# Second block of a two-block window-attention kernel: MLP input turned ahead of the attention mix, next group's input turned behind the projection, x1 in two buffers

## Chip, core and metric

The kernel runs on 1 core of one Trainium2 chip. The metric is the device time of one execution in microseconds (us). In the text, TensorE is PE, VectorE is DVE, ScalarE is ACT, GpSimd is POOL, and SyncE, which only issues DMAs here, is SP.

## What is computed

Two transformer blocks in a row over 32 images of 56 x 56 pixels with 96 channels, in float32. The first (swin) has shifted windows of 7 x 7 and normalises behind its branches. The second, which the change touches, is this:

```python
def _L1_conv_ref(x, g1, b1, w_qkv, b_qkv, w_proj, b_proj, g2, b2, w_fc1, b_fc1, w_fc2, b_fc2):
    shortcut = x
    xn = layernorm(x, g1, b1)
    windows, Hp, Wp = window_partition(xn, WS)       # WS = 8: windows of 64 pixels
    attn_out = attention(windows, w_qkv, b_qkv, w_proj, b_proj)   # 6 heads of 16
    attn_out = window_unpartition(attn_out, WS, Hp, Wp, H, W)
    x = shortcut + attn_out
    h = layernorm(x, g2, b2)
    h = jax.nn.gelu(jnp.einsum('bhwc,cd->bhwd', h, w_fc1) + b_fc1, approximate=False)
    h = jnp.einsum('bhwc,cd->bhwd', h, w_fc2) + b_fc2     # 96 -> 384 -> 96
    return x + h
```

## The kernel before

`two_blocks` runs `swin_block` into a DRAM scratch tensor and then `plain_block` from it to the output. `plain_block` cuts its 1568 windows into 196 groups of 8 windows (4 pairs of 128 pixels). Its work is a software pipeline written out by hand. Each engine has a `body(g, phase)` that lists its steps in order; a step's argument is the distance of its group from g, so in one body the scores are those of group g, the keys and queries those of g+1, the mix that of g-1, the projection that of g-2, the first MLP layer that of g-3, the second that of g-4, and the moments of the input those of g+3. An engine works its list strictly in order. Nothing but semaphores ties the engines: `wait_ge(did[...], upto(group))` waits until a step has been done for that group. Bodies are unrolled 36-fold in a loop.

The steps that matter here, in the order in which a group's data pass through them:

- **Norm of the input.** DVE takes the moments (`partial_x`, `moments_x`, L1483 and L1492). POOL makes the power -1/2 of the variance (`power_x`, L1537 and L1540), then centres and scales (`norm_x`, L1552 and L1555) into `x_norm`. PE turns that to feature-major in the one PSUM bank `psT` (`turn_x`, L1282), ACT copies it out in whole and in a high part (`copy_x`, `high_x`), DVE makes the low part (`low_x`, L1499).
- **Attention.** PE makes keys, queries and values. DVE adds the bias of the keys (`bias_k`, L1436), and SP spreads them with 6 DMAs over the partitions (`spread`, L1158). PE makes the scores (L1211), which needs all 6. DVE subtracts each row's greatest score (`shift`, L1423 and L1425), ACT takes exponentials, DVE sums for two pairs of windows at a time and inverts (`total`, L1456 and L1459), POOL scales (`scale_probs`, L1546). PE turns the probabilities through the one bank `psP` (L1232) with ACT copying out (L1332), then multiplies with the values (`mix`, L1223) and projects (`project`, L1259).
- **Residual and second norm.** DVE adds (`residual`, L1451) into `x1`. The same chain of moments (`partial_x1`, `moments_x1`), `power_x1` (L1567, L1570), `norm_x1` (L1576, L1579), `turn_x1` (L1291, through the same `psT`), `high_x1` on ACT and `low_x1` (L1430) on DVE follows. POOL also makes `x1_res` from `x1` (`residual_x1`, L1561) and `x_res` from the loaded input (`residual_x`, L1531).
- **MLP.** PE `hidden` in 3 chunks (L1191 to L1193), ACT GELU, PE `output` (L1273), DVE `result` (L1414), SP `store`.

SP's list for a number n is `load(n)`, `spread(n - 2)`, `store(n - 8)`, all in one queue. `load(n)`, which has 4 DMAs, first waits for `x_res` of group n-2, because that group's `x_in` buffer is overwritten:

```python
def load(n, parity):
    sp.wait_ge(did['x_res'], upto(n - 2))
    sp.wait_ge(did['x_norm'], upto(n - 2))
```

So the keys of group g+1 are spread behind the load of g+3, and that behind `residual_x(1)` in POOL's body of g.

Of the kernel before, what the change touches and what calls it, by code (L numbers as in the profile page):

```python
# [40 lines left out]
PAIRS = 4  # L41
# [918 lines left out]
def plain_block(nc, cfg, src, dst, par, const, psum):  # L960
# [14 lines left out]
    with ctx:  # L975
# [47 lines left out]
        mixedT = sb('mixedT', [DIM + 1, 2, NT])  # L1023
        x1 = sb('x1', [TT, PAIRS, DIM])
        x1_res = sb('x1_res', [TT, 4, PAIRS, DIM])
# [106 lines left out]
        with nc.Block() as block:  # L1132
# [50 lines left out]
            def _(pe):  # L1183

                def body(g, phase):
# [90 lines left out]
                    def turn_x(d):  # L1276
                        if exists(g + d, groups):
                            pe.wait_ge(did['x_norm'], upto(g + d))
                            pe.wait_ge(did['x1T_low'], upto(g - 4))
                            pe.wait_ge(did['xT'], upto(g + d - 1))  # L1280
                            for p in range(PAIRS):
                                last = nc.tensor.transpose(psT[0:DIM, p * TT:(p + 1) * TT], x_norm[:, p, :], ident[0:TT, 0:TT])  # L1282
                            last.then_inc(did['x_turned'], 1)

                    def turn_x1(d):
                        if exists(g + d, groups):
                            pe.wait_ge(did['x1_norm'], upto(g + d))
                            pe.wait_ge(did['xT'], upto(g + 2))
                            pe.wait_ge(did['x1T_low'], upto(g + d - 1))
                            for p in range(PAIRS):  # L1290
                                last = nc.tensor.transpose(psT[0:DIM, p * TT:(p + 1) * TT], x1_norm[:, p, :], ident[0:TT, 0:TT])  # L1291
                            last.then_inc(did['x1_turned'], 1)
# [7 lines left out]
                    turn_probs(-1, 3)  # L1300
                    turn_x(2)
                    mix(-1)
# [3 lines left out]
                    project(-2, B)  # L1306
                    turn_x1(-3)
                    free(('v_heads', 1), ('k_hat', 1), ('hid', -4, 1, CHUNKS), ('x2', -5))
# [12 lines left out]
            def _(act):  # L1321

                def body(g, phase):
# [58 lines left out]
                    copy_turned(-1, 3)  # L1382
                    copy_x(2)
                    high_x(2)
                    exponentials(0, 1)
                    copy_mixed(-1)
                    spread_values(1, A)
                    exponentials(0, 2)
                    high_x1(-3)
                    exponentials(0, 3)  # L1390
# [10 lines left out]
            def _(dve):  # L1401

                def body(g, phase):
# [40 lines left out]
                    def residual(d, bank):  # L1444
                        if exists(g + d, groups):
                            dve.wait_ge(did['proj_made'], upto(g + d))
                            dve.wait_ge(did['x_res'], upto(g + d))
                            dve.wait_ge(did['x1_norm'], upto(g + d - 1))
                            dve.wait_ge(did['x1_res'], upto(g + d - 1))
                            made = psM[:, bank, 0:PAIRS * DIM].rearrange('p (n c) -> p n c', c=DIM)  # L1450
                            nc.vector.tensor_tensor(x1[:, :, :], made, x_res[:, (phase + d) % 4], ALU.add).then_inc(did['x1'], 1)  # L1451

# [8 lines left out]
                    def partial_x1(d):  # L1461
                        if exists(g + d, groups):
                            dve.wait_ge(did['x1'], upto(g + d))
                            dve.wait_ge(did['moments2'], upto(g + d - 1))
                            for p in range(PAIRS):
                                last = nc.vector.bn_stats(stats2[:, p, :], x1[:, p, :])
                            last.then_inc(did['stats2'], 1)
# [37 lines left out]
                    shift(0, 2)  # L1505
                    shift(0, 3)
                    residual(-2, B)
                    total(0, 0)
                    low_x1(-3)
                    partial_x1(-2)  # L1510
# [9 lines left out]
            def _(pool):  # L1520

                def body(g, phase):
# [34 lines left out]
                    def residual_x1(d):  # L1557
                        if exists(g + d, groups):
                            pool.wait_ge(did['x1'], upto(g + d))
                            pool.wait_ge(did['x2'], upto(g + d - 4))  # L1560
                            nc.gpsimd.tensor_tensor(x1_res[:, (phase + d) % 4], x1[:, :, :], bcast(row_fc2[0:TT, :], 1, PAIRS), ALU.add).then_inc(did['x1_res'], 1)  # L1561

# [9 lines left out]
                    def norm_x1(d):  # L1572
                        if exists(g + d, groups):
                            pool.wait_ge(did['moments2'], upto(g + d))
                            pool.wait_ge(did['x1_turned'], upto(g + d - 1))
                            nc.gpsimd.tensor_tensor(x1_norm[:, :, :], x1[:, :, :], bcast(moments2[:, :, 0], 2, DIM), ALU.subtract).then_inc(did['x1_centred'], 1)  # L1576
                            pool.wait_ge(did['x1_centred'], upto(g + d))
                            pool.wait_ge(did['rstd2'], upto(g + d))
                            nc.gpsimd.tensor_tensor(x1_norm[:, :, :], x1_norm[:, :, :], bcast(rstd2[:, :], 2, DIM), ALU.mult).then_inc(did['x1_norm'], 1)  # L1579

                    power_x(2)
                    norm_x(2)
                    residual_x(1)
                    power_x1(-3)
                    norm_x1(-3)
                    residual_x1(-3)
# [85 lines left out]
```

## Time and profile before

| what | value |
|---|---|
| median of 3 runs | 7526.55 us (7525.05 to 7533.92) |
| the profiled execution | 7536.2 us, span of its instructions 7534.4 us |
| busy share of the span | PE 95%, PE weight load 73%, DVE 84%, ACT 84%, POOL 73% |
| second block | from about 4430 us to the end |

The span runs from the first to the last instruction. Busy shares are means over both blocks; an engine that waits for semaphores is not busy. A matmul's end is modelled. For this change the second block is read as one repeating period, body after body.

### The profile page before, as it was taken

To read this page: it belongs to the slowest core of one execution; us is meant where nothing else is said; L and a number is where in the kernel's file an instruction comes from. 1 tells how busy PE (TensorE), PEld (TensorE's weight loads), DVE (VectorE), ACT (ScalarE), POOL (GpSimd) and SP (SyncE) were. 2 spreads that over 40 slices of the span, in tenths; PEclk is the share of its full clock that TensorE was granted. 3 is DMA by queue.
4 is the path that set the end of the run, shared out by engine and by line. 5 is a ranking of instruction groups with operands and counts; after the bars stand their busy time and mean duration, and the time that the engine had idled before them with its cause. 6 is when DMAs were issued, how large, how long until landed. Compare 5 with 4: busy or idle time off the path is not lost. (4 is left out here: it accounts for less than half of the span.)

```text
span 7534.4 us, 313308 instructions
## 1 busy us (share of the span) xinstructions
PE 7125.2 (95%) x110894; PEld 5485.8 (73%) x110894; DVE 6291.5 (84%) x13110; ACT 6293.5 (84%) x11444; POOL 5480.2 (73%) x6349
## 2 busy tenths in 40 slices
PE   7999999999999999999999968999999999998998
PEld 4777777777777777777777757777777777777777
DVE  5888888888888888888888857887887887887886
ACT  5999999999999999999999957777777777777776
POOL 3777777777777777777777756776776776776775
PEclk9999999999999999999999979999999999999999
DMA  0111111111111111111111111111111111111111
GB/s 21 30 29 30 30 30 29 29 30 30 30 29 30 30 30 30 29 30 30 30 29 30 29 24 36 41 42 40 41 41 40 41 41 40 41 41 40 42 41 34
DMA packets 379978, 252.67 MB, mean 34 GB/s; under 512 B 284184, under 2 KB 359704, under 8 KB 378520
## 3 DMA queue, kind: packets, MB, share of 16 engines
q1 hardware_dynamic: 378522, 233.09, 12.6%
q8 instruction: 934, 15.30, 0.9%
q14 instruction: 522, 4.28, 0.2%
HBM read 78.64 MB, written 77.07 MB: 21 GB/s over the span
## 5 line engine op out<-in xcount | busy, mean ns | idle before, releaser
L879 POOL TENSOR_TENSOR swin_score<-swin_score,swin_top 113x588 f32<-113x588 f32 x1024 | 1204.6, 1176 | 741.0 <-DVE swin_top L751 740.3
L1546 POOL TENSOR_TENSOR plain_prob<-plain_prob,plain_inv_total 128x384 f32<-128x384 f32 x784 | 635.0, 831 | 671.6 <-DVE plain_inv_total L1459 671.6
L622 ACT ACTIVATE swin_probT<-swin_ps_probs 128x339 f32<-128x339 f32 x2048 | 924.4, 451 | 196.1 <-PE swin_ps_probs L479 176.1
L479 PE MATMUL swin_ps_probs<-swin_ident,swin_prob 113*128 113x113 f32 x6144 | 991.2, 270 | 7.1 <-ACT swin_probT L622 7.1
L479 PEld LDWEIGHTS swin_ps_probs<-swin_ident,swin_prob 113*128 113x128 f32 x6144 | 667.8, 141 | 355.1 <-issue 321.6
L746 DVE TENSOR_TENSOR swin_score<-swin_ps_scores,swin_bias_tab 113x588 f32<-113x588 f32 x1024 | 777.2, 759 | 173.9 <-PE swin_ps_scores L469 172.6
L751 DVE TENSOR_REDUCE swin_top<-swin_score 113x12 f32<-113x588 f32 x1024 | 769.1, 751 | 0.2
L628 ACT ACTIVATE swin_prob<-swin_score 113x588 f32<-113x588 f32 x1024 | 719.2, 702 | 5.8 <-POOL swin_score L879 2.9
L1344 ACT ACTIVATE plain_hid<-plain_ps_dense,plain_b_fc 128x512 f32<-128x512 f32 x588 | 404.3, 688 | 340.1 <-PE plain_ps_dense L1193 322.1
L782 DVE SCALAR_TENSOR_TENSOR swin_x<-swin_y,swin_y_rstd,swin_x_res 98x96 f32<-98x96 f32 x1024 | 603.1, 646 | 0.8 <-POOL swin_y_rstd L897 0.7
L493 PEld LDWEIGHTS swin_ps_mixed<-swin_probT,swin_v_heads 128*32 128x32 f32 x24576 | 422.5, 109 | 223.2 <-issue 145.8
L469 PE MATMUL swin_ps_scores<-swin_k_heads,swin_q_hat 32*64 32x196 f32 (+1 forms) x12288 | 577.7, 347 | 4.9 <-DVE swin_score L746 4.9
L562 PE MATMUL swin_ps_dense<-swin_w_fc,swin_hid 128*98 128x96 f32 x6144 | 575.7, 250 | 1.2 <-ACT swin_hid L699 1.2
L493 PE MATMUL swin_ps_mixed<-swin_probT,swin_v_heads 128*32 128x49 f32 x24576 | 563.1, 210 | 2.3 <-ACT swin_probT L622 1.0
L562 PEld LDWEIGHTS swin_ps_dense<-swin_w_fc,swin_hid 128*98 128x98 f32 x6144 | 557.6, 167 | 1.5 <-ACT swin_hid L699 1.5
L1273 PE MATMUL plain_ps_dense<-plain_w_fc,plain_hid 128*128 128x96 f32 x4704 | 557.3, 275 | 1.1 <-ACT plain_hid L1344 1.1
L1332 ACT ACTIVATE plain_probT<-plain_ps_probs 128x384 f32<-128x384 f32 x784 | 383.1, 489 | 202.5 <-PE plain_ps_probs L1232 202.3
L1273 PEld LDWEIGHTS plain_ps_dense<-plain_w_fc,plain_hid 128*128 128x128 f32 x4704 | 546.1, 193 | 1.6 <-ACT plain_hid L1344 1.6
L1451 DVE TENSOR_TENSOR plain_x<-plain_ps_dense,plain_x_res 128x384 f32<-128x384 f32 x196 | 109.2, 557 | 487.3 <-POOL plain_x_res L1561 458.9
L885 POOL TENSOR_TENSOR swin_x_res<-swin_x_in,swin_res_row 98x384 f32<-98x384 f32 x256 | 256.2, 1001 | 290.5 <-DVE swin_x L782 235.1
L1423 DVE TENSOR_REDUCE plain_top<-plain_ps_scores 128x6 f32<-128x384 f32 x784 | 425.1, 542 | 45.0 <-PE plain_ps_scores L1211 44.6
L1425 DVE TENSOR_TENSOR plain_score<-plain_ps_scores,plain_top 128x384 f32<-128x384 f32 x784 | 437.0, 557 | 26.9
(185 smaller groups left out, 21081.0 us busy)
## 6 DMA issues: line engine op xcount, KB each, us to landing
swin_k_heads<-swin_k_hat SPq DMA_DIRECT2D x1024, 36.8 KB
plain_x_in<-between_blocks SPq DMA_DIRECT2D x784, 48.0 KB, 2.2
plain_k_heads<-plain_k_hat SPq DMA_DIRECT2D x1176, 32.0 KB, 2.0
out_dram<-plain_x SPq DMA_DIRECT2D x784, 48.0 KB
swin_x_in<-in_x SPq DMA_DIRECT2D x224, 136.5 KB
between_blocks<-swin_x SPq DMA_DIRECT2D x224, 136.5 KB
swin_x_in<-in_x SPq DMA_DIRECT2D x224, 19.5 KB
between_blocks<-swin_x SPq DMA_DIRECT2D x224, 19.5 KB
```

The source lines that it names most:

```text
L469: last = nc.tensor.matmul(psS[half * HALF:half * HALF + rows, band, 0:BC], q_hat[part, parity(d), w * WIN:w * WIN + rows], k_heads[part, p ...
L479: last = nc.tensor.transpose(psP[:, n * QT:(n + 1) * QT], prob[0:QT, p, 2 * hp:2 * hp + 2, :].rearrange('p h k -> p (h k)'), ident[0:QT, 0 ...
L493: last = nc.tensor.matmul(psO[32 * band:32 * band + 32, first:first + WIN], v_heads[:, (phase + d) % 4, 2 * p + half, band, n, :], probT[: ...
L562: last = nc.tensor.matmul(psM[0:TT, bank, p * DIM:(p + 1) * DIM], hid[:, c, p * TT:(p + 1) * TT], w_fc2[:, c, :], start=c == 0, stop=c == ...
L622: nc.scalar.activation(to, psP[:, 0:3 * QT], ACT.Copy).then_inc(did['probT'], 1)
L628: nc.scalar.activation(prob[0:QT, p, :, 0:WIN], score[0:QT, p % 2, :].rearrange('p (h k) -> p h k', k=WIN), ACT.Exp).then_inc(did['prob'], 1)
L746: nc.vector.tensor_tensor(score[0:QT, p % 2, :].rearrange('p (b n) -> p b n', b=BANDS), psS[0:QT, :, 0:BC], kind, ALU.add).then_inc(did['s ...
L751: nc.vector.tensor_reduce(top[0:QT, p % 2, :], score[0:QT, p % 2, :].rearrange('p (h k) -> p h k', k=WIN), AX.X, ALU.max).then_inc(did['to ...
L782: last = nc.vector.scalar_tensor_tensor(x1[:, p, :], y[:, p, :], y_rstd[:, p:p + 1], x_res[:, (phase + d) % 4, p, :], ALU.mult, ALU.add)
L879: nc.gpsimd.tensor_tensor(view, view, bcast(top[0:QT, p % 2, :], 2, WIN), ALU.subtract).then_inc(did['shifted'], 1)
L1273: last = nc.tensor.matmul(psM[0:TT, bank, p * DIM:(p + 1) * DIM], hid[:, c, p * TT:(p + 1) * TT], w_fc2[:, c, :], start=c == 0, stop=c == ...
L1546: nc.gpsimd.tensor_tensor(pair, pair, bcast(inv_total[0:QT, p // 2, p % 2 * heads:(p % 2 + 1) * heads], 2, WIN), ALU.mult).then_inc(did['p ...
```

## The change

In `plain_block` alone, with the same instructions in number and shape as before:

- `x1` has two buffers, so `residual(d)` waits for `x1_norm` and `x1_res` of two groups back and not of the one before.
- PE turns the MLP input (`turn_x1(-3)`) ahead of the mix, where the next input (`turn_x(2)`) was turned, and turns the next input behind the projection, where the MLP input was. ACT's copies of the two change places likewise.
- POOL does the chain of the second norm ahead of that of the first; `residual_x(1)`, which stood between the two chains, now stands behind both.
- DVE does `low_x1(-3)` ahead of `residual(-2)` and of the first `total`.

```diff
--- before.py
+++ after.py
@@ -1021,7 +1021,7 @@
         total_of = sb('total', [128, 2, 2 * heads])
         inv_total = sb('inv_total', [128, 2, 2 * heads])
         mixedT = sb('mixedT', [DIM + 1, 2, NT])
-        x1 = sb('x1', [TT, PAIRS, DIM])
+        x1 = sb('x1', [TT, 2, PAIRS, DIM])
         x1_res = sb('x1_res', [TT, 4, PAIRS, DIM])
         x1T_high = sb('x1T_high', [DIM, NT], F32R)
         x1T_low = sb('x1T_low', [DIM, NT], F32R)
@@ -1276,7 +1276,7 @@
                     def turn_x(d):
                         if exists(g + d, groups):
                             pe.wait_ge(did['x_norm'], upto(g + d))
-                            pe.wait_ge(did['x1T_low'], upto(g - 4))
+                            pe.wait_ge(did['x1T_low'], upto(g - 3))
                             pe.wait_ge(did['xT'], upto(g + d - 1))
                             for p in range(PAIRS):
                                 last = nc.tensor.transpose(psT[0:DIM, p * TT:(p + 1) * TT], x_norm[:, p, :], ident[0:TT, 0:TT])
@@ -1285,7 +1285,7 @@
                     def turn_x1(d):
                         if exists(g + d, groups):
                             pe.wait_ge(did['x1_norm'], upto(g + d))
-                            pe.wait_ge(did['xT'], upto(g + 2))
+                            pe.wait_ge(did['xT'], upto(g + 1))
                             pe.wait_ge(did['x1T_low'], upto(g + d - 1))
                             for p in range(PAIRS):
                                 last = nc.tensor.transpose(psT[0:DIM, p * TT:(p + 1) * TT], x1_norm[:, p, :], ident[0:TT, 0:TT])
@@ -1298,13 +1298,13 @@
                     free(('hid', -4, 2, CHUNKS), ('x1', -3), ('q_hat', 0))
                     queries(1, B)
                     turn_probs(-1, 3)
-                    turn_x(2)
+                    turn_x1(-3)
                     mix(-1)
                     free(('k_hat', 1), ('hid', -4, 1, CHUNKS), ('x2', -5), ('v_heads', 0))
                     values(1, A)
                     free(('q_hat', 1), ('hid', -4, 2, CHUNKS), ('x1', -3))
                     project(-2, B)
-                    turn_x1(-3)
+                    turn_x(2)
                     free(('v_heads', 1), ('k_hat', 1), ('hid', -4, 1, CHUNKS), ('x2', -5))
                     output(-4, A)
                     free(('x1', -2), ('q_hat', 1), ('hid', -4, 2, CHUNKS))
@@ -1380,13 +1380,13 @@
                     copy_turned(-1, 2)
                     exponentials(0, 0)
                     copy_turned(-1, 3)
-                    copy_x(2)
-                    high_x(2)
+                    high_x1(-3)
                     exponentials(0, 1)
                     copy_mixed(-1)
                     spread_values(1, A)
                     exponentials(0, 2)
-                    high_x1(-3)
+                    copy_x(2)
+                    high_x(2)
                     exponentials(0, 3)
                     act.preload_act_table_set(GELU_SET)
                     gelu(-3, 0, B)
@@ -1445,10 +1445,10 @@
                         if exists(g + d, groups):
                             dve.wait_ge(did['proj_made'], upto(g + d))
                             dve.wait_ge(did['x_res'], upto(g + d))
-                            dve.wait_ge(did['x1_norm'], upto(g + d - 1))
-                            dve.wait_ge(did['x1_res'], upto(g + d - 1))
+                            dve.wait_ge(did['x1_norm'], upto(g + d - 2))
+                            dve.wait_ge(did['x1_res'], upto(g + d - 2))
                             made = psM[:, bank, 0:PAIRS * DIM].rearrange('p (n c) -> p n c', c=DIM)
-                            nc.vector.tensor_tensor(x1[:, :, :], made, x_res[:, (phase + d) % 4], ALU.add).then_inc(did['x1'], 1)
+                            nc.vector.tensor_tensor(x1[:, parity(d)], made, x_res[:, (phase + d) % 4], ALU.add).then_inc(did['x1'], 1)
 
                     def total(d, h):
                         if exists(g + d, groups):
@@ -1463,7 +1463,7 @@
                             dve.wait_ge(did['x1'], upto(g + d))
                             dve.wait_ge(did['moments2'], upto(g + d - 1))
                             for p in range(PAIRS):
-                                last = nc.vector.bn_stats(stats2[:, p, :], x1[:, p, :])
+                                last = nc.vector.bn_stats(stats2[:, p, :], x1[:, parity(d), p, :])
                             last.then_inc(did['stats2'], 1)
                             dve.wait_ge(did['stats2'], upto(g + d))
                             dve.wait_ge(did['var_eps2'], upto(g + d - 1))
@@ -1504,9 +1504,9 @@
                     bias_q(1, B)
                     shift(0, 2)
                     shift(0, 3)
+                    low_x1(-3)
                     residual(-2, B)
                     total(0, 0)
-                    low_x1(-3)
                     partial_x1(-2)
                     result(-4, A)
                     total(0, 1)
@@ -1558,7 +1558,7 @@
                         if exists(g + d, groups):
                             pool.wait_ge(did['x1'], upto(g + d))
                             pool.wait_ge(did['x2'], upto(g + d - 4))
-                            nc.gpsimd.tensor_tensor(x1_res[:, (phase + d) % 4], x1[:, :, :], bcast(row_fc2[0:TT, :], 1, PAIRS), ALU.add).then_inc(did['x1_res'], 1)
+                            nc.gpsimd.tensor_tensor(x1_res[:, (phase + d) % 4], x1[:, parity(d)], bcast(row_fc2[0:TT, :], 1, PAIRS), ALU.add).then_inc(did['x1_res'], 1)
 
                     def power_x1(d):
                         if exists(g + d, groups):
@@ -1573,16 +1573,16 @@
                         if exists(g + d, groups):
                             pool.wait_ge(did['moments2'], upto(g + d))
                             pool.wait_ge(did['x1_turned'], upto(g + d - 1))
-                            nc.gpsimd.tensor_tensor(x1_norm[:, :, :], x1[:, :, :], bcast(moments2[:, :, 0], 2, DIM), ALU.subtract).then_inc(did['x1_centred'], 1)
+                            nc.gpsimd.tensor_tensor(x1_norm[:, :, :], x1[:, parity(d)], bcast(moments2[:, :, 0], 2, DIM), ALU.subtract).then_inc(did['x1_centred'], 1)
                             pool.wait_ge(did['x1_centred'], upto(g + d))
                             pool.wait_ge(did['rstd2'], upto(g + d))
                             nc.gpsimd.tensor_tensor(x1_norm[:, :, :], x1_norm[:, :, :], bcast(rstd2[:, :], 2, DIM), ALU.mult).then_inc(did['x1_norm'], 1)
 
+                    power_x1(-3)
+                    norm_x1(-3)
                     power_x(2)
                     norm_x(2)
                     residual_x(1)
-                    power_x1(-3)
-                    norm_x1(-3)
                     residual_x1(-3)
                     scale_probs(0, 0)
                     scale_probs(0, 1)
```

PE's list in one body, from the last turned pair of the group before to the second MLP layer (`plain_ps_turn` is `psT`; L1282 turns the input, L1291 the MLP input). Before:

```order
L1232 MATMUL plain_ps_probs<-plain_ident,plain_prob 128x128 x3
L1278 REGISTER_ALU
L1282 MATMUL plain_ps_turn<-plain_ident,plain_x_norm 96x128 x4
L1223 MATMUL plain_ps_mixed<-plain_probT,plain_v_heads 32x64 x24
L1252 MATMUL plain_ps_dense<-plain_w_qkv,plain_xT 64x48 x16
L1259 MATMUL plain_ps_dense<-plain_w_proj,plain_mixedT 128x96 x4
L1291 MATMUL plain_ps_turn<-plain_ident,plain_x_norm 96x128 x4
L1273 MATMUL plain_ps_dense<-plain_w_fc,plain_hid 128x96 x12
```

The same stretch of the change:

```order
L1232 MATMUL plain_ps_probs<-plain_ident,plain_prob 128x128 x3
L1291 MATMUL plain_ps_turn<-plain_ident,plain_x_norm 96x128 x4
L1223 MATMUL plain_ps_mixed<-plain_probT,plain_v_heads 32x64 x24
L1252 MATMUL plain_ps_dense<-plain_w_qkv,plain_xT 64x48 x16
L1259 MATMUL plain_ps_dense<-plain_w_proj,plain_mixedT 128x96 x4
L1278 REGISTER_ALU
L1282 MATMUL plain_ps_turn<-plain_ident,plain_x_norm 96x128 x4
L1273 MATMUL plain_ps_dense<-plain_w_fc,plain_hid 128x96 x12
```

The two turns have changed places; the rest stands as it did.

POOL's list from the start of a body to `residual_x1` (L1561), behind which the four scalings of L1546 follow (`plain_x_res` in L1531 is `x_res`, in L1561 it is `x1_res`). Before:

```order
L1537 TENSOR_TENSOR plain_var_eps<-plain_moments,plain_epsilon 128x4
L1540 TENSOR_TENSOR plain_rstd<-plain_var_eps,plain_half_power 128x4
L1552 TENSOR_TENSOR plain_x_norm<-plain_x_in,plain_moments 128x384
L1555 TENSOR_TENSOR plain_x_norm<-plain_x_norm,plain_rstd 128x384
L1529 ISA
L1531 TENSOR_TENSOR plain_x_res<-plain_x_in,plain_res_row 128x384
L1567 TENSOR_TENSOR plain_var_eps<-plain_moments,plain_epsilon 128x4
L1570 TENSOR_TENSOR plain_rstd<-plain_var_eps,plain_half_power 128x4
L1576 TENSOR_TENSOR plain_x_norm<-plain_x,plain_moments 128x384
L1579 TENSOR_TENSOR plain_x_norm<-plain_x_norm,plain_rstd 128x384
L1561 TENSOR_TENSOR plain_x_res<-plain_x,plain_row_fc 128x384
```

The same stretch of the change:

```order
L1567 TENSOR_TENSOR plain_var_eps<-plain_moments,plain_epsilon 128x4
L1570 TENSOR_TENSOR plain_rstd<-plain_var_eps,plain_half_power 128x4
L1576 TENSOR_TENSOR plain_x_norm<-plain_x,plain_moments 128x384
L1579 TENSOR_TENSOR plain_x_norm<-plain_x_norm,plain_rstd 128x384
L1535 REGISTER_ALU
L1537 TENSOR_TENSOR plain_var_eps<-plain_moments,plain_epsilon 128x4
L1540 TENSOR_TENSOR plain_rstd<-plain_var_eps,plain_half_power 128x4
L1552 TENSOR_TENSOR plain_x_norm<-plain_x_in,plain_moments 128x384
L1555 TENSOR_TENSOR plain_x_norm<-plain_x_norm,plain_rstd 128x384
L1529 ISA
L1531 TENSOR_TENSOR plain_x_res<-plain_x_in,plain_res_row 128x384
L1561 TENSOR_TENSOR plain_x_res<-plain_x,plain_row_fc 128x384
```

L1531, on which SP's load waits, was sixth in the list and is now behind both chains of four.

## Rows read from the trace of the kernel before

**Rows 1.** The head of the profile page.

```profile
span 7534.4 us, 313308 instructions
```

**Rows 2.** Waits, 4600 to 7500 us: waiter, awaited, total us, times, longest us.

```profile
DVE plain_x L1451 <- POOL plain_x_res L1561: 449.6, 182, 2.6
...
POOL plain_var_eps L1537 <- DVE plain_moments L1492: 170.6, 185, 1.3
...
PE plain_ps_scores L1211 <- DMA plain_k_heads<-plain_k_hat: 20.6, 39, 1.5
```

**Rows 3.** Timeline over one period: start us, us, engine, line, what [idle before].

```profile
6006.58 1.12 PE L1211 MATMUL plain_ps_scores<-plain_k_heads,plain_q_hat 32*64 32x128 f32 x48
...
6007.89 0.20 POOL L1537 TENSOR_TENSOR plain_var_eps<-plain_moments,plain_epsilon 128x4 f32<-128x4 f32 x1 [0.91 <-DVE plain_moments L1492]
...
6010.13 0.49 ACT L1332 ACTIVATE plain_probT<-plain_ps_probs 128x384 f32<-128x384 f32 x1 [0.29 <-PE plain_ps_probs L1232]
...
6010.85 1.00 POOL L1531 TENSOR_TENSOR plain_x_res<-plain_x_in,plain_res_row 128x384 f32<-128x384 f32 x1
...
6011.52 1.09 PE L1223 MATMUL plain_ps_mixed<-plain_probT,plain_v_heads 128*32 128x64 f32 x48
...
6012.27 4.06 SPq L1150 DMA_DIRECT2D plain_x_in<-between_blocks  x4
...
6012.85 0.56 DVE L1425 TENSOR_TENSOR plain_score<-plain_ps_scores,plain_top 128x384 f32<-128x384 f32 x1
...
6013.61 1.13 PE L1259 MATMUL plain_ps_dense<-plain_w_proj,plain_mixedT 96*128 96x96 f32 x8
...
6014.76 1.00 POOL L1561 TENSOR_TENSOR plain_x_res<-plain_x,plain_row_fc 128x384 f32<-128x384 f32 x1
...
6014.86 0.64 PE L1291 MATMUL plain_ps_turn<-plain_ident,plain_x_norm 128*96 128x128 f32 x4
...
6015.34 2.82 PE L1273 MATMUL plain_ps_dense<-plain_w_fc,plain_hid 128*128 128x96 f32 x24
...
6015.90 0.56 DVE L1451 TENSOR_TENSOR plain_x<-plain_ps_dense,plain_x_res 128x384 f32<-128x384 f32 x1 [2.49 <-POOL plain_x_res L1561]
...
6016.47 3.77 SPq L1158 DMA_DIRECT2D plain_k_heads<-plain_k_hat  x6
...
6017.49 0.62 DVE L1430 TENSOR_TENSOR plain_x1T_low<-plain_ps_turn,plain_x1T_high 96x512 fp32r<-96x512 f32 x1
...
6018.26 0.47 PE L1191 MATMUL plain_ps_dense<-plain_x1T_high,plain_w_fc_high 96*128 96x512 f32 x1
...
6018.79 0.56 DVE L1414 TENSOR_TENSOR plain_x<-plain_ps_dense,plain_x_res 128x384 f32<-128x384 f32 x1
...
6020.55 1.62 POOL L1546 TENSOR_TENSOR plain_prob<-plain_prob,plain_inv_total 128x384 f32<-128x384 f32 x2 [1.28 <-DVE plain_inv_total L1459]
...
6021.36 1.35 DVE L1499 TENSOR_TENSOR plain_xT_low<-plain_xT,plain_xT_high 96x512 fp32r<-96x512 f32 x1
...
6021.73 1.12 PE L1211 MATMUL plain_ps_scores<-plain_k_heads,plain_q_hat 32*64 32x128 f32 x48
...
6023.08 0.20 POOL L1537 TENSOR_TENSOR plain_var_eps<-plain_moments,plain_epsilon 128x4 f32<-128x4 f32 x1 [0.92 <-DVE plain_moments L1492]
```

**Rows 4.** Timeline of SP's queue in the next period.

```profile
6027.50 3.62 SPq L1150 DMA_DIRECT2D plain_x_in<-between_blocks  x4
6031.28 3.79 SPq L1158 DMA_DIRECT2D plain_k_heads<-plain_k_hat  x6
```

**Rows 5.** The spread's tile, 4600 to 7500 us: durations in ns, and landing.

```profile
L1158 SPq DMA_DIRECT2D plain_k_heads<-plain_k_hat x1128: 507/589/1812, 4601.2 to 7469.5; - x188
...
DMA to landing us min/median/max: 1.9/2.0/3.8
```

**Rows 6.** Timeline in the first block, around one low part on DVE.

```profile
2003.01 1.08 DVE L836 TENSOR_TENSOR swin_xT_low<-swin_xT,swin_xT_high 96x392 fp32r<-96x392 f32 x1
...
2003.62 0.53 POOL L921 TENSOR_TENSOR swin_z_eps<-swin_z_var,swin_epsilon_sum 98x4 f32<-98x4 f32 x1
```

## The prediction

> **What bounds the kernel now.** I read the page for the span first: 7534.4 us [rows 1]; the profiled execution's own time is 7536.2, and the median of the runs shown is 7526.55, some 10 us less, so I add differences to the median. The change touches only the second block. There the timeline repeats every 15.19 us: the scores start at 6006.58 and 6021.73, POOL's body at 6007.89 and 6023.08 [rows 3]. (The scores jitter by some hundredths, POOL's start less, so 15.19 is the period.) About 182 groups run in this rhythm, as many as wait in the same place [rows 2].
>
> The view of waits names two that form a ring. DVE's residual waits for POOL's `x1_res` 182 times, 2.5 us each; POOL's first step waits for DVE's moments of the input 185 times, 0.9 us each [rows 2]. The timeline shows the ring closed: POOL works from 6007.89 without a gap to the end of L1561 at 6015.76; DVE's residual starts 0.14 behind it and DVE then works without a stop until its moments release POOL at 6023.08 [rows 3]. That is 7.87 + 0.14 + 7.18 = 15.19. The ring exists because `x1` has one buffer.
>
> A second path is nearly as long. Spreading the keys is queued on SP behind the load, and the load waits for `x_res`. In the period shown, L1531 ends at 6011.85, the load is issued from 6012.27, the 6 spreading DMAs from 6016.47 to 6020.24 [rows 3]. The last is issued 0.59 before that end and lands 2.0 after its start [rows 5], 1.41 behind the end; with 0.08 for TensorE to pick it up that is 6021.73, when the scores start. So this period was already held by the DMA. In the next one the same path gives 6027.50 + 3.62 and 6031.28 + 3.79 = 6035.07 [rows 4], + 1.49 = 6036.56, behind `x_res` at 6023.08 + 3.96 = 6027.04: 9.52 us. From `x_res` to the scores this path thus takes 9.88 and 9.52 us, mean 9.70. TensorE is seen waiting for this DMA 39 times, 20.6 us in all [rows 2]: the path has some tenths of slack at most.
>
> **The change, part by part.** All times from here on are counted from the start of the scores of g (6006.58 is 0).
>
> *x1 in two buffers.* The residual no longer waits for POOL; it waits for the projection. The ring above is gone. The projection ends at 6014.74 now [rows 3], at 8.16, before L1561's end at 9.18. Behind the residual in DVE's list stand both totals, `result` and all the moments, so all of them may move ahead until TensorE holds them.
>
> *TensorE's list.* The MLP input's turn takes the place in which the input's turn waited for POOL. Its `x1_norm` is there early (below), so it falls in the gap before the mix. The mix then waits only for ACT's last copy of turned probabilities, which ends at 6010.62 [rows 3], at 4.04; with 0.11 for the pick-up the mix starts at 4.15 and not 4.94. From the mix to the projection's end is 3.22 us (6011.52 to 6014.74), so that is at 7.37. The input's turn, now next, must find `psT` free: `low_x1` follows `shift(0, 3)`, which ends at 6013.41 [rows 3], at 6.83, and takes 0.62, so 7.4. Turn at 7.45. From the turn before the second MLP layer to that layer's end is 3.30 us (6014.86 to 6018.16), so 10.75.
>
> *DVE.* `result` starts at 10.8, when that layer is done; the residual, the first total and the partial moments fit before it (from 7.4 they need 6018.75 - 6015.90 = 2.85 less the 0.6 of `low_x1`), so DVE idles a little over 1 us there. That is the new wait, and behind it stand the second total, the moments and `low_x`; POOL's last two scalings wait for the total. From `result` to those scalings is 6018.79 to 6020.55, 1.76 us, and they take 1.62: they end at 14.18. Before it was 6022.17, at 15.59. The change has moved this point 1.41 us ahead.
>
> *POOL.* Before, `x_res` came from the start of the body at 6023.08 (16.50), 3.96 us later, at 20.46. Now the second norm's chain and only then the first's stand before it. The first costs 2.91 us (from 6011.85 to the start of L1561 at 6014.76), the other with `x_res` 3.96 as before: from 14.18 that is 21.05.
>
> *The collision.* `low_x` on DVE has both inputs in SBUF, and takes 1.35 us. It starts at 6021.36 while POOL scales, and ends 0.54 behind POOL's end at 6022.17 [rows 3]: it was held until POOL had finished. Now POOL has its next step ready at that moment, which it hadn't before. In the first block such a meeting is seen: while DVE's low part runs to 2004.09, POOL's 4-element step of 0.20 us (as L1537 in rows 3) takes 0.53 and ends at 2004.15 [rows 6], 0.06 behind DVE. Here POOL's first step would end 0.54 + 0.06 behind the scalings and not 0.17: 0.43 lost. Bounds: 0, if POOL goes first and DVE slips into a gap, and 0.54, all of DVE's run. I take 0.43, since the row is of the same meeting. `x_res` is then at 21.48, and with it everything behind it on SP.
>
> The Trainium skill ("SBUF — State Buffer", Who interferes with whom) says that a VectorE instruction with two SBUF inputs and a GpSimd instruction that reads SBUF exclude each other, and that the later one blocks fully. By that rule POOL would lose all 0.54, and the total would be 10 us more than mine; the 1.35 us of `low_x` agree with it, and it doesn't say who goes first when both wait.
>
> *The sum.* The `x_res` that follows the scores of g is that of g+2, because POOL's next body makes it; SP loads g+4 behind it and then spreads g+2. So the scores of g+2 start 21.48 + 9.70 = 31.18 after those of g: 15.59 per group against 15.19. Before it was 20.46 + 9.92 = 30.38. In short, `x_res` comes 1.02 later and the slack was 0.2. 182 groups x 0.40 = 73 us: 7526.55 + 73 = 7600. The norm of x1 is then ready 14.18 + 0.43 + 2.96 - 15.59 = 2.0 us behind the next scores, ahead of its turn at 3.3, so it is no limit. ACT has the same steps and waits for the same producers; the second buffer itself costs nothing. Filling and draining are left as they are.
>
> **Rivals.**
>
> *1 (forecast): the spread of the keys binds; slower.* For it: the 9.5 us from `x_res` are SP's own issue times, which the change doesn't touch. Its own range: without the collision and with 9.52, (21.05 + 9.52) / 2 = 15.29, 7544 us; with 0.54 lost, 10.0 behind `x_res` (single spreads took up to 1812 ns and landings up to 3.8 us [rows 5], which slack hid until now) and another 0.4 on TensorE's waits, 16.0, 7673 us. Chance 0.70.
>
> *2: TensorE's list binds; faster.* If the keys were there in time, the scores could follow the first MLP layer: that ran from 6018.26 to the scores at 6021.73, 3.47 us, and starts 0.1 behind the output: 10.75 + 3.57 = 14.32, which gives 182 x -0.87 = -158 and 7368 us. It needs 9.7 to be 7.2, or `x_res` 2.5 earlier. Any gain at all needs 21.48 + 9.70 to fall under 30.38, so 0.8 us that I have put on the ring but that isn't on it. Against it: SP's issues alone are 0.42 + 4.20 + 3.77 = 8.4. Chance 0.13 with the partial gains between, which give 7400 to 7500.
>
> *3: no difference.* The ring of x1 is gone and the key path takes over at the same length: no collision, the shorter path, and TensorE a little sooner. 30.4 / 2 = 15.2, 7527 us. Chance 0.12.
>
> *4: more is lost than the first's range holds*, by waits that alternate between SP's jitter and TensorE: over 7673, at 7690 say. Chance 0.05.
>
> **How the numbers follow.** The predicted time is the first's, 7600. A measurement of this kernel tells about 0.2%, 15 us, from no change. Slower: 0.70 and 0.05, and a part of the third's spread, 0.77; faster 0.13; same 0.10. The range leaves out the second (0.13) and the end above: 7535 to 7670.
>
> **What would show it.** Right: POOL's wait for the moments gone, DVE's wait at L1451 gone and one of about 1.3 us at L1414 for L1273 in its place; TensorE waiting over 1 us for the spread in nearly all groups; a period near 15.6. The mix at 4.15 and the second MLP layer's end at 10.75 behind the scores, `x_res` at 21.5. L1537 or L1567 right behind the scalings with some 0.5 us and not 0.20 shows the collision. Wrong: TensorE busy through to the scores, with a period under 15.19; or `x_res` to scores under 9 us.

## The result: 7818 us, slower by 3.85%

The changed kernel takes 7818.11 us (median of 4 runs, 7808.36 to 7830.11) against 7528.09 for the one before in the same count of runs: a ratio of 1.0385, 95% interval 1.0367 to 1.0403. The prediction's direction was right and its size was not: 7600, with a range to 7670. The profiled execution is one of 7814.75 us.

The page of the changed kernel shows it in one line besides the span. The row PEclk is the granted clock of TensorE in 40 slices, in tenths: 9 in all slices but one before, but here 8 in some of those of the second block.

```profile
span 7812.9 us, 313325 instructions
...
PE 7258.8 (93%) x110894; PEld 5647.4 (72%) x110894; DVE 6258.8 (80%) x13110; ACT 6315.3 (81%) x11444; POOL 5552.6 (71%) x6349
...
PEclk9999999999999999999999889988999989998999
```

The stretch 5000 to 7000 us, first of the kernel before and then of the change (us, then busy time and instructions of PE, PE weight load, DVE, ACT, POOL, then granted clock, DMA share, GB/s):

```profile
5000.00:7000.00 2000.00, 1820.42 (x25350) 1433.84 (x25349) 1610.10 (x4420) 1465.80 (x2470) 1403.29 (x1821) 0.99 0.18 41
```

```profile
5000.00:7000.00 2000.00, 1746.60 (x23164) 1411.96 (x23163) 1449.09 (x4030) 1350.15 (x2254) 1327.26 (x1663) 0.90 0.16 37
```

The mean clock falls from 0.99 to 0.90, and every engine does less in the same time. The view of waits between 4600 and 7780 us (waiter, awaited, total us, times, longest us) answers to [rows 2]: neither of the ring's two waits is in it any more.

```profile
PE plain_ps_scores L1211 <- DMA plain_k_heads<-plain_k_hat: 321.1, 91, 6.5
DVE plain_x L1414 <- PE plain_ps_dense L1273: 207.3, 189, 1.3
...
DVE plain_x L1451 <- PE plain_ps_dense L1259: 149.2, 188, 2.0
```

TensorE waits for the spread keys in 91 groups, 3.5 us each and 6.5 at most: about every other group. That is the alternation which the timeline shows. Below are one late group and its successors (start us, us, engine, line, what, [idle before]); the columns are those of [rows 3].

```profile
6503.35 0.65 POOL L1567 TENSOR_TENSOR plain_var_eps<-plain_moments,plain_epsilon 128x4 f32<-128x4 f32 x1
...
6506.07 1.27 PE L1211 MATMUL plain_ps_scores<-plain_k_heads,plain_q_hat 32*64 32x128 f32 x48 [3.27 <-DMA plain_k_heads<-plain_k_hat]
...
6507.81 0.63 PE L1192 MATMUL plain_ps_dense<-plain_xT_low,plain_w_qk_high 96*96 96x512 f32 x1
...
6511.17 3.62 SPq L1150 DMA_DIRECT2D plain_x_in<-between_blocks  x4
...
6512.21 1.80 PE L1223 MATMUL plain_ps_mixed<-plain_probT,plain_v_heads 128*32 128x64 f32 x48
...
6514.95 3.79 SPq L1158 DMA_DIRECT2D plain_k_heads<-plain_k_hat  x6
...
6516.41 2.82 PE L1273 MATMUL plain_ps_dense<-plain_w_fc,plain_hid 128*128 128x96 f32 x24
...
6519.63 0.56 DVE L1414 TENSOR_TENSOR plain_x<-plain_ps_dense,plain_x_res 128x384 f32<-128x384 f32 x1 [1.19 <-PE plain_ps_dense L1273]
...
6521.39 1.61 POOL L1546 TENSOR_TENSOR plain_prob<-plain_prob,plain_inv_total 128x384 f32<-128x384 f32 x2 [1.84 <-DVE plain_inv_total L1459]
...
6522.46 1.12 PE L1211 MATMUL plain_ps_scores<-plain_k_heads,plain_q_hat 32*64 32x128 f32 x48
...
6522.96 0.65 POOL L1567 TENSOR_TENSOR plain_var_eps<-plain_moments,plain_epsilon 128x4 f32<-128x4 f32 x1
...
6529.32 1.00 POOL L1531 TENSOR_TENSOR plain_x_res<-plain_x_in,plain_res_row 128x384 f32<-128x384 f32 x1
```

```profile
6534.57 3.77 SPq L1158 DMA_DIRECT2D plain_k_heads<-plain_k_hat  x6
...
6539.82 1.12 PE L1211 MATMUL plain_ps_scores<-plain_k_heads,plain_q_hat 32*64 32x128 f32 x48 [3.27 <-DMA plain_k_heads<-plain_k_hat]
```

The scores of 6506.07 waited, and those of 6539.82 again waited 3.27 us. The scores of 6522.46 between them did not wait. So the keys bind every second group, and the pair takes 33.75 us, not twice 15.59. The row of POOL's first step, one per group, gives the mean: 183 starts from 4611.8 to 7681.6 us, 16.9 us apart.

```profile
L1567 POOL TENSOR_TENSOR plain_var_eps<-plain_moments,plain_epsilon x183: 198/648/722, 4611.8 to 7681.6; 128x4 f32<-128x4 f32 x183
```

The last view is of windows in that pair: behind the wait, on to the second of the scores, and one group further (columns as above).

```profile
6507.20:6513.90 6.70, 6.70 (x70) 5.18 (x64) 5.80 (x11) 2.40 (x5) 4.39 (x5) 0.51 0.15 36
6514.00:6522.40 8.40, 8.40 (x85) 7.08 (x83) 5.21 (x20) 7.00 (x12) 2.63 (x4) 1.00 0.22 50
6522.40:6536.00 13.60, 13.13 (x195) 10.73 (x195) 11.52 (x30) 10.94 (x19) 10.68 (x14) 1.00 0.11 25
```

For 6.7 us behind the wait TensorE has a clock of 0.51, the lower of its two levels, 1.2 GHz. In the two windows that follow it has 1.00. In the timeline a 96x512 product (L1192) takes 0.63 us there, and the mix 1.80 us against 1.09 in [rows 3].

The Trainium skill ("TensorE: Matmul & The Clock Gate", HAM oscillation) describes this course: waits for a DMA let the clock drop at each step of a loop, so that each next stretch begins slow. By that rule the clock should have been among my rivals; the trace agrees with it, 0.51 behind the wait of 3.3 us.

The trace of the kernel before shows the same course, and I passed over it. Once in 36 groups, where the unrolled loop turns, the scores come late: at 5161.34, 5715.19, 6268.25 and 6821.50 us, by 3.3 to 3.6 us each. Behind each the clock is at its lower level for 6.7 us or more. Here is the second of the four with its window (the profile names nothing that it waited for):

```profile
5715.19 1.21 PE L1211 MATMUL plain_ps_scores<-plain_k_heads,plain_q_hat 32*64 32x128 f32 x48 [3.34 <-issue]
```

```profile
5716.20:5722.90 6.70, 6.70 (x71) 5.18 (x64) 5.58 (x10) 2.79 (x6) 5.10 (x7) 0.50 0.15 32
```

### The profile page after: what moved, and what is told of

Same layout as the page of the kernel before. It is cut to its first block and busy times, and to the rows that moved or that the text cites. A ratio compares the mean times of both kernels' runs of the same rounds, so it can differ in the third digit from the quotient of the medians.

```text
span 7812.9 us, 313325 instructions
## 1 busy us (share of the span) xinstructions
PE 7258.8 (93%) x110894; PEld 5647.4 (72%) x110894; DVE 6258.8 (80%) x13110; ACT 6315.3 (81%) x11444; POOL 5552.6 (71%) x6349
## 5 line engine op out<-in xcount | busy, mean ns | idle before, releaser
L1546 POOL TENSOR_TENSOR plain_prob<-plain_prob,plain_inv_total 128x384 f32<-128x384 f32 x784 | 635.0, 831 | 1054.5 <-DVE plain_inv_total L1459 1054.5
L1211 PE MATMUL plain_ps_scores<-plain_k_heads,plain_q_hat 32*64 32x128 f32 x9408 | 278.8, 324 | 341.0 <-DMA plain_k_heads<-plain_k_hat 327.9
L1232 PEld LDWEIGHTS plain_ps_probs<-plain_ident,plain_prob 128*128 128x128 f32 x2352 | 333.9, 161 | 260.2 <-issue 187.7
L1211 PEld LDWEIGHTS plain_ps_scores<-plain_k_heads,plain_q_hat 32*64 32x64 f32 x9408 | 218.8, 159 | 419.0 <-issue 419.0
```

What stands on the lines that cost most here:

```text
L1546: nc.gpsimd.tensor_tensor(pair, pair, bcast(inv_total[0:QT, p // 2, p % 2 * heads:(p % 2 + 1) * heads], 2, WIN), ALU.mult).then_inc(did['p ...
```

## Experiments

**The keys' path.** Two ways to bring `x_res` sooner, both with TensorE's, ACT's and DVE's lists as changed. The first moves it between POOL's two chains:

```diff
                     power_x1(-3)
                     norm_x1(-3)
+                    residual_x(1)
                     power_x(2)
                     norm_x(2)
-                    residual_x(1)
                     residual_x1(-3)
```

> The change, with POOL's residual_x(1) moved up from behind both norm chains to between them. Theory 1 (the keys are late because x_res stands behind both chains, and TensorE's clock halves after its wait of over 3 us in every other group): x_res comes 2.96 us sooner, two groups then need 33.6 - 3.0 - 2.4 (the clock stays up) = 28.2 us by the key path, and TensorE's own list binds at 14.1 to 14.4 per group, without alternation: about 7370 us. Theory 2 (TensorE's new order of turns is what costs, by the pair's 33.6 us; the late keys only fill its slack): the period stays near 16.8 and the time near 7818. Theory 3 (half: keys late, the clock a matter apart that stays low): 15.3 to 15.6 per group, 7550 to 7600.

Measured: 7390.94 us, ratio to the kernel before 0.9816 (0.9800 to 0.9833). The alternation is gone and 427 us with it. Theory 2 falls: TensorE's new order is not the cost. The keys are still at the edge, though:

```profile
PE plain_ps_scores L1211 <- DMA plain_k_heads<-plain_k_hat: 51.4, 84, 1.8
```

The second makes `x_res` a group earlier, in a gap of POOL:

```diff
-                    residual_x(1)
                     residual_x1(-3)
                     scale_probs(0, 0)
                     scale_probs(0, 1)
+                    residual_x(2)
                     scale_probs(0, 2)
```

> The change, with x_res of the next group (residual_x(2)) made in POOL's wait of 1.85 us between the second and the third scaling, and not behind both chains. Theory 1: x_res comes 6 us or more sooner, the key path has slack of over 2 us per group, and the time is that of the run with x_res between the chains, about 7370, or up to 20 us lower if that run still waits for keys here and there. Theory 2: near 7818. If the key path were still the bound with x_res between the chains, this run would be clearly faster than that one.

Measured: 7303.21 us, 0.9698 (0.9682 to 0.9714). That is 88 us less than the run with `x_res` between the chains, so that one was indeed still held by the keys; my "up to 20" was too small. The group starts every 14.03 us. SP no longer waits for `x_res` but for the keys themselves:

```profile
SPq L1154 <- DVE plain_k_hat L1436: 194.1, 181, 6.1
SPq L1150 <- POOL plain_x_res L1531: 1.6, 3, 0.8
```

In its timeline the load is issued before the scores, and the spread starts 4.3 us behind their start:

```profile
6501.03 1.01 POOL L1531 TENSOR_TENSOR plain_x_res<-plain_x_in,plain_res_row 128x384 f32<-128x384 f32 x1
...
6502.61 3.64 SPq L1150 DMA_DIRECT2D plain_x_in<-between_blocks  x4
...
6503.87 1.12 PE L1211 MATMUL plain_ps_scores<-plain_k_heads,plain_q_hat 32*64 32x128 f32 x48
...
6508.14 4.49 SPq L1158 DMA_DIRECT2D plain_k_heads<-plain_k_hat  x6
...
6517.90 0.35 PE L1211 MATMUL plain_ps_scores<-plain_k_heads,plain_q_hat 32*64 32x128 f32 x6
```

(The last row is cut short by the end of the stretch that was read.)

**The order on SP.** The change with `x_res` left late, and only SP's loop altered:

```diff
-                        load(2 * m + k, k)
                         spread(2 * m + k - 2, k)
+                        load(2 * m + k, k)
                         store(2 * m + k - 8, k)
```

> The change, with SP's loop in another order: the spread of the keys is issued ahead of the load and not behind it. x_res stays behind both chains on POOL. Theory 1 (x_res is late, and it matters only because the keys are queued behind the load that waits for it): the keys land by 10 us behind the scores, TensorE's list and the ring through the norm of x1 bind as in the run with x_res in POOL's gap, 14.0 us per group and 7300 to 7330. If the late load itself binds too (DVE's moments of the input wait for it, 93 times before): 14.1 to 14.6, up to 7420. If the order on SP doesn't matter: 7818.

Measured: 7429.64 us, 0.9868 (0.9850 to 0.9885). Exchanging two entries of a queue gives 388 us. The keys' place behind the load is the mechanism. The late load then binds in its turn, which puts the time 10 us above the second case (up to 7420):

```profile
DVE plain_stats L1483 <- DMA plain_x_in<-between_blocks: 214.4, 179, 2.0
```

**The clock.** Dummy transposes of a constant keep TensorE at work ahead of the scores. They add work and take none away:

```diff
                     hidden(-3, 2, B)
+                    filler(9)   # 9 times matmul(psO[96:128, 0:128], ident[:, 0:32], ident[:, :])
```

> The change, with 9 dummy transposes of a constant (128x128 against 32 columns, into the unused partitions 96 to 127 of the bank of the mix) at the end of TensorE's list in each body, about 1.2 us, which fills the wait ahead of the scores; nothing of the computation is left out. Theory 1: TensorE's longest wait shrinks below 1 us, the clock stays at 1.00, the alternation goes, and the period is that of the key path at full clock, (21.5 + 0.35 + 9.7) / 2 = 15.8, 7640 us: work added, 180 us gained. Theory 2 (TensorE's list is the cost): 1.2 us more in each group, about 8040. If the clock is only a mark of the waits and costs nothing: unchanged at 7818.

Measured: 7710.56 us, 1.0241 (1.0224 to 1.0258), 108 us less than the change. The 9 took 2.1 us and not 1.2, so TensorE's list (16.0 us) became the bound and 7640 could not be reached. The clock and the waits for the keys:

```profile
5000.00:7000.00 2000.00, 1917.37 (x26057) 1575.43 (x26056) 1520.49 (x4155) 1384.86 (x2320) 1367.46 (x1715) 0.99 0.17 39
```

```profile
PE plain_ps_scores L1211 <- DMA plain_k_heads<-plain_k_hat: 19.4, 40, 1.0
```

With 4 of them:

> As the run with 9 dummy transposes, with 4 of them, about 0.95 us per group by their measured 2.1 us for 9. TensorE's own list then takes about 15.0 us, below the key path. Theory 1 (the key path at full clock, with the result 0.35 us later than in the prediction, is the bound): the clock stays up, and the period is (21.85 + 9.7) / 2 = 15.8 us, 7640 us, between the changed kernel's 7818 and its value without lateness. Rival (the run with 9 was faster only because a longer list keeps the groups evenly apart, and with 4 they drift apart again): alternation comes back and the time is 7750 to 7820.

Measured: 7691.47 us, 1.0216 (1.0199 to 1.0233). I had expected 7640; the rival, 7750 to 7820, is about as far off. Waits of up to 4.2 us and some lower clock were left:

```profile
PE plain_ps_scores L1211 <- DMA plain_k_heads<-plain_k_hat: 148.4, 107, 4.2
```

```profile
5000.00:7000.00 2000.00, 1827.94 (x24918) 1478.10 (x24904) 1528.56 (x4166) 1390.68 (x2331) 1369.52 (x1716) 0.97 0.17 39
```

With 6:

> As the runs with 9 and 4 dummy transposes, with 6: TensorE's own list takes about 15.4 us (9 made it 16.0, 4 made it 14.9). In the run with 4, pairs of groups in which nothing else happened took 14.91 + 16.38 = 31.29 us, 15.65 each, while others took up to 19.3 in one. Theory 1 (at full clock the key path of the change is 15.6 to 15.7 per group, as predicted, and everything above it is the clock after long waits): with the list at 15.4 no wait can exceed about 1 us, the clock stays at 0.99, the period is 15.7 and the time 7600 to 7650, below both other runs of this kind. If the path itself is longer than I hold: between the two others, 7690 to 7710.

Measured: 7648.40 us, 1.0163 (1.0145 to 1.0181): the lowest of the three, as theory 1 said, at the upper edge of its range. No wait is over 2.0 us and the mean clock is 1.00:

```profile
PE plain_ps_scores L1211 <- DMA plain_k_heads<-plain_k_hat: 93.4, 106, 2.0
```

```profile
5000.00:7000.00 2000.00, 1874.37 (x25865) 1525.33 (x25865) 1553.68 (x4248) 1415.28 (x2373) 1396.73 (x1750) 1.00 0.17 39
```

It isn't at full clock throughout: four times in these 2000 us it falls to the lower level for 3.4 us. One of them is behind the longest wait:

```profile
5764.30:5767.60 3.30, 3.30 (x14) 2.66 (x12) 3.21 (x6) 1.38 (x3) 3.14 (x5) 0.50 0.01 1
```

Everywhere else this run shows the change's keys' path at full clock. From a group whose scores didn't wait to one two groups on whose scores did (times of the scores, mix, second layer, `result` on DVE, last scalings, POOL's first step; and then `x_res`, spread and scores of two groups on):

```profile
5311.41 1.12 PE L1211 MATMUL plain_ps_scores<-plain_k_heads,plain_q_hat 32*64 32x128 f32 x48
...
5315.53 1.09 PE L1223 MATMUL plain_ps_mixed<-plain_probT,plain_v_heads 128*32 128x64 f32 x48 [0.19 <-issue]
...
5319.39 2.82 PE L1273 MATMUL plain_ps_dense<-plain_w_fc,plain_hid 128*128 128x96 f32 x24
...
5322.61 0.56 DVE L1419 TENSOR_TENSOR plain_x<-plain_ps_dense,plain_x_res 128x384 f32<-128x384 f32 x1 [1.55 <-PE plain_ps_dense L1273]
...
5324.37 1.61 POOL L1551 TENSOR_TENSOR plain_prob<-plain_prob,plain_inv_total 128x384 f32<-128x384 f32 x2 [2.20 <-DVE plain_inv_total L1464]
...
5325.94 0.65 POOL L1572 TENSOR_TENSOR plain_var_eps<-plain_moments,plain_epsilon 128x4 f32<-128x4 f32 x1
```

```profile
5332.30 1.00 POOL L1536 TENSOR_TENSOR plain_x_res<-plain_x_in,plain_res_row 128x384 f32<-128x384 f32 x1
...
5337.55 3.77 SPq L1158 DMA_DIRECT2D plain_k_heads<-plain_k_hat  x6
...
5344.43 1.12 PE L1211 MATMUL plain_ps_scores<-plain_k_heads,plain_q_hat 32*64 32x128 f32 x48 [1.02 <-DMA plain_k_heads<-plain_k_hat]
```

**The two buffers of x1.** The kernel before with them and nothing else:

> The kernel before with x1 in two buffers and nothing else. The wait of DVE for POOL (2.5 us per group) goes. Theory 1: the key path of before (x_res 3.96 us after the start of POOL's body) has only 0.2 us of slack, but DVE's moments and so POOL's body come earlier with it; the next bounds are the input's turn ahead of the mix and the second norm's late turn: 14.6 to 15.1 per group, 7420 to 7510. If the second buffer were itself the harm (Theory 4: a looser order lets groups drift apart until the keys are late): slower than 7528, towards 7818.

Measured: 7468.10 us, 0.9919 (0.9903 to 0.9936), with a median period of 14.87. By itself the buffer is a gain of 60 us; theory 4 falls. Then the run with `x_res` in POOL's gap, with one buffer:

> The run with x_res in POOL's gap, with x1 back in one buffer. There x1_res is done at 6511.75 and the residual starts at 6511.73, so a single buffer would hold it by some 0.2 us, and DVE waits over 1 us for TensorE behind it. If the order of the turns and of POOL made the gain and the second buffer none: within 15 us of 7303. If the buffer is what took the old ring away also here: 7400 or more.

Measured: 7303.68 us, 0.9704 (0.9688 to 0.9721), the same as with two. Once the second norm is done early, the buffer is worth nothing: the wait that it removes is hidden.

**The collision on the shared port.** The change, with the low part read from PSUM (both turns then wait for `xT_low` and no longer for `xT`, since it must be read before the bank is overwritten):

```diff
-nc.vector.tensor_tensor(xT_low[:, parity(d), :], xT[0:DIM, parity(d), 0:NT], xT_high...
+nc.vector.tensor_tensor(xT_low[:, parity(d), :], psT[0:DIM, 0:NT], xT_high...
```

> The change, with DVE's low part of the input read from PSUM and its high part from SBUF, in place of both from SBUF (same values; the turn of the MLP input waits for it). Then DVE's instruction should take 0.6 us and not up to 1.35, and POOL's first step behind the scalings 0.2 and not 0.65. Theory 1: the key path gets 0.45 shorter over two groups, 182 x 0.22 = 40 us, 7778, with the alternation and the half clock still there. If the collision costs nothing on the path: 7818.

Measured: 7765.60 us, 1.0323 (1.0306 to 1.0340), 52 us less, where 40 were expected. The same edit on the run with `x_res` in the gap:

> The run with x_res in POOL's gap, with DVE's low part of the input read from PSUM. There the ring is: turn of the MLP input, mix, projection, the input's turn, second layer, result, total, scalings, POOL's chain for x1, and the turn waits for it 0.6 us; the collision's 0.45 is on it once per group. Theory: 14.03 - 0.45 = 13.6 us, 7303 - 80 = 7225. Rival: TensorE's own list, with its waits for the single bank of turned probabilities, binds just below 14.0, and the gain is under 30 us.

Measured: 7282.22 us, 0.9674 (0.9658 to 0.9690). This is the best version: 3.3% under the kernel before. Both instructions are as short as expected:

```profile
L1499 DVE TENSOR_TENSOR plain_xT_low<-plain_ps_turn,plain_xT_high x185: 685/687/689, 4604.4 to 7191.0; 96x512 fp32r<-96x512 f32 x185
```

```profile
L1567 POOL TENSOR_TENSOR plain_var_eps<-plain_moments,plain_epsilon x185: 198/202/207, 4605.1 to 7191.7; 128x4 f32<-128x4 f32 x185
```

But the gain is 21 us and not 80: the rival was right in size, though it named another wait. The MLP input's turn and the mix come 0.45 us sooner behind the scores (median 3.57 and 4.15, against 4.02 and 4.60), but the input's turn only 0.13 (7.53 against 7.66). It needs DVE's `low_x1`, which ends at 6509.18, 0.10 before it. That this is what holds it is read from the timeline, and no edit tests it:

```profile
6505.32 0.64 PE L1291 MATMUL plain_ps_turn<-plain_ident,plain_x_norm 128*96 128x128 f32 x4
...
6509.28 0.61 PE L1282 MATMUL plain_ps_turn<-plain_ident,plain_x_norm 128*96 128x128 f32 x4 [0.16 <-issue]
```

```profile
6508.50 0.68 DVE L1430 TENSOR_TENSOR plain_x1T_low<-plain_ps_turn,plain_x1T_high 96x512 fp32r<-96x512 f32 x1
```

## Why the prediction was right and wrong

**Right: the old ring and its end.** DVE's wait for `x1_res` and POOL's for the moments are gone, DVE waits 1.1 us for the second layer (207.3 us in 189 groups; predicted 1.3), and the buffer alone gives 60 us.

**Right: what takes its place.** The keys, queued on SP behind the load that waits for `x_res`. Three edits of this path (7391, 7303 and 7430 us), the last of them in SP's list alone, turn the loss into a gain. Rival 2, a faster kernel, was right about the place where TensorE's list would bind: 14.03 us per group with `x_res` in the gap, predicted 14.32. It was right only without the keys' lateness.

**Right: the terms of the sum at full clock.** In the run with 6 dummies the mix starts 4.12 behind the scores (predicted 4.15), the second layer ends at 10.80 (10.75), and POOL's first step ends 0.61 us behind the scalings (0.60). From the scalings' end at 5325.98 to `x_res` at 5333.30 are 7.32 us (7.30).

**Mis-sized: from the second layer to `result`.** I let DVE start 0.05 us behind the modelled end of the matmuls. In the two groups shown it starts 0.40 behind (5322.21 to 5322.61, and 6519.23 to 6519.63 in the change); in three quarters of the groups of either run it is 0.30. So in the pair shown `x_res` comes 21.89 behind the scores and not 21.48, and over the run with 6 dummies the median is 21.79: 0.31 more, 182 x 0.31 / 2 = 28 us.

**Mis-sized: the path from `x_res` to the scores.** 9.70 was nearly the floor. One of its two readings, 9.52, ended at a landing that I had worked out; the scores of that period start 0.35 later, at 6036.91. In the change the path took 9.50 in the pair shown (median 9.52), but in the pair of the run with 6 dummies 11.1, with the spread issued by 5341.32 and the scores 3.11 behind it and not 1.49. The median there, over the 111 groups whose scores waited, is 10.11. That is 0.41 over my term, 37 us if every pair had it. Not every pair waits, and the run as a whole is at 7648 us, 48 above my 7600. Why the keys land later there than in the change, no run here tests.

**The step that failed: "So the scores of g+2 start 21.48 + 9.70 = 31.18 after those of g: 15.59 per group".** Its form holds: in the late chain of the change the pair is 24.25 + 9.50 = 33.75. What doesn't hold is the term for TensorE's list inside it, the second layer's end at 10.75. I took it from a loop at full clock and put it behind waits for the keys that my own sum had made, as if those were idle time and nothing more. It also took the waits as evenly shared.

The path runs from the scores of g to those of g+2, so even and odd groups are two chains, tied only by TensorE's list. Nothing keeps them evenly apart: one can follow the other by the 14.0 us of the list, and then the other chain carries all the waiting of both, 3.3 us in one place instead of the 1.3 in each (15.59 - 14.32) that I had counted on. Behind it TensorE runs at the lower clock, the list of the late group takes 2.4 us more (second layer done at 13.16 behind the scores, against 10.80), and `x_res` comes at 24.25 instead of 21.89. In the pair shown 16.39 us pass from the late scores to the next, the list at the lower clock, and then 14.09 of list and 3.27 of wait. The lateness feeds itself, since the late chain is slowed and the other not.

An estimate from these rows is 91 late groups x 2.36 = 215 us. The run with 6 dummies shows the size: 7648 with the mean clock at 1.00 against 7818, 170 of the 218 us by which I was wrong.

What starts the alternation, in a loop whose groups are all alike, no run here singles out; waits of over 3 us in every second group are there from 4581 us on, some six groups into the block. That the fillers also change the spacing by lengthening the list is part of each of them, so the share of the clock alone and that of the uneven spacing weren't told apart. The pairs' own sum says that at full clock uneven spacing costs nothing: in the run with 4 dummies groups of 14.9 and 16.4 us follow each other, 31.3 together.

**The range** held rival 1 to 7673 with everything late at once, but always at full clock. Rival 4 named alternating waits and more loss than that, with a chance of 0.05 and 7690 as its time; it had no lower clock in it either. I read only the mean clock of the kernel before, 0.99. Its four late scores with half the clock behind them were in the same trace and showed what a wait of over 3 us is followed by.

## What to carry to other kernels

When a buffer removes a ring of waits, follow each queue that is served in order to the next thing that is late: here a constant row's sum on POOL held a load, and the load held keys that had been ready for 4.7 us. Issue what is urgent before what waits, or make what it waits for in a gap of its producer. A dependence that reaches over two iterations must be read as two chains: their mean says what they cost only if no resource punishes one long wait more than two short ones, and TensorE's clock does. What one long wait is followed by can often be read before the change is made: here the loop's turn showed it once in 36 groups.

## What the runs showed that I hadn't expected

- Adding 1.5 us of useless matmuls per group to TensorE, the busiest engine, made the kernel 170 us faster (7818 to 7648).
- A wait of 3.3 us is followed by 6.7 us at clock 0.51; with waits of at most 2.0 us the mean clock over 2000 us was 1.00, four stretches of 3.4 us at 0.50 included.
- When DVE's instruction with two SBUF inputs and POOL's next step both wait for POOL's current one, DVE went first in the median group, as I read it from the durations: POOL's 4-element step took 0.648 us and not 0.20, and 0.202 in the run without the second SBUF input. The Trainium skill ("SBUF — State Buffer", Who interferes with whom) says that whoever issues first holds the shared pair, but not who goes next when both wait behind a third; these runs agree with the exclusion.
- DVE begins 0.30 us, in one group of four 0.40, behind the modelled end of a row of accumulating matmuls, in the change and in the run with 6 dummies alike.
